# Six plain FFN groups and ten by 7 products, with the attention pairs placed in half steps

## The chip, the cores and the metric

The kernel runs on one core of a Trainium2 chip. Its time is the device time of one execution in microseconds (us); the number of a kernel is the median of several runs. The engines are TensorE (PE, matmuls; PEld is its weight load), VectorE (DVE), ScalarE (ACT), GpSimd (POOL) and SyncE (SP), which here only issues DMA transfers. They run their own instruction lists in order and wait for each other through semaphores. Sixteen DMA engines move data.

## The reference

One layer with gates on x of shape (64, 128, 512), f32, and a context of the same shape:

```python
x = x + tanh(g_xattn) * attention(layernorm(x), ctx, ctx)
x = x + tanh(g_ffn) * ffn(layernorm(x))

# attention: A is a fixed 128x128 matrix of each of 4 heads, summed over all 64 batches, V = ctx @ Wh
O = einsum('hst,bthe->bshe', A, V)
Y = (O - mean) / sqrt(var + 1e-3) * gamma + beta
W = relu(x @ wg_w)
return (W * Y) @ wo_w

# ffn, ternary weights, 512 -> 1408 -> 512
g = (x @ gate_w.T) * gate_s
u = (x @ up_w.T) * up_s
return (silu(g) * u) @ down_w.T * down_s
```

## The kernel before

A tile is one batch of 128 rows by 512, so there are 64 tiles, 32 pairs of tiles (q = 0 to 31) and 16 groups of four tiles. An f32 operand is split into a high and a low f16 part, and a product is made from two or three matmuls.

The first stage (to about 360 us) computes V, the gates W and the sums for A, and stores V and W in scratch memory. A short transition handles the first two pairs of tiles fully. From then on the FFN runs in two stages.

**The plain stage** has NS = 8 groups. Each has 15 steps, n = 15 g + step. Steps 0 to 10 are gate/up steps: `up_mm` issues 8 matmuls for gate and 8 for up of 128 hidden columns (L2067), `silu` on ACT (L907) and `hidden` on DVE (L1436) form the hidden values, `hidden_hi` (ACT, L836) and `hidden_lo` (POOL, L1816) split them. Steps 11 to 14 are down steps: `down_mm` issues 22 matmuls for one tile (L2074) and `finish` on DVE adds the residual. Two PSUM slots alternate between steps: a step on PE waits for `hidden` or `finish` of the step two before.

Beside these steps the rest of the attention is computed, pair by pair, each event of a pair at a fixed step of every engine's list. For pair q: `o` (PE, A times V, L1930), `y_stats` (DVE, L1252) and `y_rstd_pair` (POOL); `y_normal` (ACT); `y_blocks` (DVE, 32x32 transposes), `y_out` (SP, to scratch), `y_in` (SP, back in pieces of 128 bytes, which makes it a whole transpose, L510); `w_load` (SP, L407); `y_pair_affine` (ACT, four instructions, L786); `wy_pair_mul` (DVE, L1284); `wy_pair_hi` (ACT, L825) and `wy_pair_lo` (POOL, L1760), which make the two parts of W * Y; `wo_pair` (PE, 16 matmuls on the high part at L2058, 8 on the low part at L2062); `x1` and `stats2` (DVE, L1295, L1299, L1301); `norm2_pair` (ACT); `x2_blocks` (DVE), `x2_out` and `x1_store` (SP). `v_load`, `v_hi`, `v_lo` bring in V two pairs ahead, `x_again` brings in x. Most of the buffers exist once: `y_in` of a pair waits for the product of the pair before, `w_load` for its `wy_pair_lo`. The FFN groups read x2 back by `x2_in`, again in pieces of 128 bytes.

What sets the places is `pieces(n)`: it lists the pairs and which event (piece 0 to 12) of each is due at step n. Pair q starts at step `first_step(q)`, one every 3.5 steps, rounded down:

```python
def first_step(q):
    return 7 * (q - 3) // 2 + 1 if q > 3 else 2 * q - 6
# piece 0 o, stats, v_hi; 1 normal, v_lo; 2 blocks, v_load; 3 y_out; 4 y_in; 5 w_load; 6 affine
# piece 7 mul, hi, lo, x_again; 9 wo, x1, stats2; 10 norm2; 11 x2_blocks; 12 x2_out, x1_store
```

In the same stage the weights for the second scheme are prepared: eleven times `stage_load`, `stage_residue` (POOL), `stage_store`, one every 8 steps, and six `weights_copy`.

**The stage of 7 products** has NP = 4 pairs of groups. A Strassen-Winograd scheme on 2x2 blocks forms gate and up of two groups by 7 products in place of 8: `seven` issues 28 matmuls for each of the 11 column blocks (loaded as `wbuf`), DVE, ACT and POOL add the products, then 8 tiles of 22 down matmuls follow. `pair_in` loads x2 of a pair of tiles in pieces of 128 bytes, four of them for each pair of groups.

## Time and profile before

| what | value |
|---|---|
| median of the 3 runs | 1440.71 us (1440.6 to 1444.61) |
| span of the profiled execution | 1447.4 us |
| own time of the profiled execution | not given apart from its span |
| PE, DVE, ACT, POOL busy | 98%, 72%, 50%, 51% of the span |
| DMA moved | 324.96 MB, mean 225 GB/s |
| plain stage, from the first gate matmul to the first of the 7 products | about 360 to 1024 us |

The span goes from the first to the last instruction of one execution, and all rows of the trace are from that one. Durations of matmuls in the trace contain the passage through the array (0.38 us for 512 columns), so their pace is read from the starts of rows that follow each other. An "idle before" belongs to the engine and names the work that ended it.

### The profile page before, as it was taken

To read this page: it belongs to the slowest core of one execution; us is meant where nothing else is said; L and a number is where in the kernel's file an instruction comes from. 1 tells how busy PE (TensorE), PEld (TensorE's weight loads), DVE (VectorE), ACT (ScalarE), POOL (GpSimd) and SP (SyncE) were. 2 spreads that over 40 slices of the span, in tenths; PEclk is the share of its full clock that TensorE was granted. 3 is DMA by queue.
4 is the path that set the end of the run, shared out by engine and by line. 5 is a ranking of instruction groups with operands and counts; after the bars stand their busy time and mean duration, and the time that the engine had idled before them with its cause. 6 is when DMAs were issued, how large, how long until landed. Compare 5 with 4: busy or idle time off the path is not lost.

```text
span 1447.4 us, 20320 instructions
## 1 busy us (share of the span) xinstructions
PE 1420.4 (98%) x7097; PEld 728.3 (50%) x7135; DVE 1043.3 (72%) x1562; ACT 726.3 (50%) x1145; POOL 735.3 (51%) x734
## 2 busy tenths in 40 slices
PE   8999999999999999999999999999999999999998
PEld 4666666665445544455444444444444444444443
DVE  7788998878477676766776677564867768768762
ACT  5566565554555635455463545534344444443442
POOL 5656769863564445444553554434137237137235
PEclk9999999999999999999999999999999999999999
DMA  8999898973878796987888897886383473572432
GB/s 275 344 336 306 292 317 318 343 251 130 276 204 263 227 276 206 260 276 210 248 274 237 264 243 222 247 252 164 112 228 115 124 224 122 139 218 98 139 109 89
DMA packets 372920, 324.96 MB, mean 225 GB/s; under 512 B 259280, under 2 KB 285264, under 8 KB 372816
## 3 DMA queue, kind: packets, MB, share of 16 engines
q1 hardware_dynamic: 355248, 291.63, 66.2%
q10 hardware_dynamic: 17568, 31.99, 6.2%
q8 instruction: 59, 0.97, 0.3%
q14 instruction: 45, 0.37, 0.1%
HBM read 209.14 MB, written 114.43 MB: 224 GB/s over the span
## 4 chain that ended last, share of the span: by engine, by line
PE 74%; DVE 10%; DMA 6%; SPq 3%; issue 3%; ACT 2%; POOL 2%; ACTq 0%; DVEq 0%; POOLq 0%
PE ps L2067 24%; PE po L2067 8%; PE pyb L1930 7%; PE ps L2074 7%; PE ptb L2074 5%; PE pyb L2074 5%; PE ps L1988 5%; PE po L1930 3%; PE pyb L2058 3%; PE ptb L2058 3%; DMA wy_scratch<-misc 2%; SPq L510 2%; DVE reg L1129 1%; PE ptb L2062 1%; PE pyb L2062 1%
## 5 line engine op out<-in xcount | busy, mean ns | idle before, releaser
L2067 PE MATMUL ps<-x2t,gate 128*128 128x512 f16 x704 | 166.6, 379 | 1.2 <-DVE tmp L1436 1.1
L1930 PE MATMUL pyb<-xnt,wgs 128*128 128x512 f16 x708 | 166.3, 380 | 1.4 <-DVE wgs L1153 1.3
L2067 PE MATMUL ps<-op,wbuf 128*128 128x512 f16 x704 | 166.3, 379 | 0.5 <-issue 0.5
L2067 PE MATMUL ps<-x2t,up 128*128 128x512 f16 x704 | 166.3, 379 | 0.0
L1800 POOL TENSOR_TENSOR p5b<-p5b,p1b 128x512 f32<-128x512 f32 x44 | 55.7, 1265 | 209.1 <-ACT p5b L860 209.1
L1816 POOL TENSOR_TENSOR hid<-tmp,hid 128x512 f16<-128x512 f32 x88 | 104.6, 1190 | 105.9 <-ACT hid L836 105.9
L2074 PE MATMUL ps<-down_first,hid 128*128 128x512 bf16 x683 | 152.4, 379 | 2.1 <-POOL hid L1816 0.8
L1811 POOL TENSOR_TENSOR hsp<-hall,hsp 128x640 f16<-128x640 f32 (+2 forms) x72 | 123.6, 1731 | 37.1 <-ACT hsp L887 37.1
L2067 PE MATMUL po<-op,wbuf 128*128 128x512 f16 x528 | 129.0, 379 | 0.6 <-DVE u2b L1383 0.6
L1436 DVE SCALAR_TENSOR_TENSOR tmp<-ps,colsb,tmp 128x512 f32<-128x512 f32 x88 | 65.4, 744 | 68.2 <-PE ps L2067 62.3
L1988 PE MATMUL ps<-reg 128*128 128x256 f32 x768 | 109.7, 294 | 4.3 <-DVE reg L1129 3.8
L2067 PEld LDWEIGHTS ps<-op,wbuf 128*128 128x128 bf16 x704 | 68.5, 98 | 84.4 <-issue 2.5
L1760 POOL TENSOR_TENSOR wy_part<-raw,wy_part 128x1024 f16<-128x1024 f32 x30 | 66.0, 2201 | 87.6 <-ACT wy_part L825 87.6
L2067 PEld LDWEIGHTS ps<-x2t,up 128*128 128x128 bf16 x704 | 68.8, 98 | 82.9
L907 ACT ACTIVATE tmp<-ps,colsb 128x512 f32<-128x512 f32 x88 | 60.3, 685 | 99.2 <-PE ps L2067 99.1
L2074 PEld LDWEIGHTS ps<-down_first,hid 128*128 128x128 f16 x704 | 68.1, 98 | 83.4 <-POOL hid L1816 2.0
L2067 PEld LDWEIGHTS ps<-x2t,gate 128*128 128x128 bf16 x704 | 67.0, 98 | 81.0 <-DVE tmp L1436 1.8
L1988 PEld LDWEIGHTS ps<-reg 128*128 128x128 f32 x768 | 98.4, 190 | 13.3 <-DVE reg L1129 5.7
L1930 PEld LDWEIGHTS pyb<-xnt,wgs 128*128 128x128 f16 x708 | 66.4, 98 | 73.7 <-DVE wgs L1153 2.6
L1721 POOL TENSOR_TENSOR reg<-raw,reg 128x512 fp32r<-128x512 f32 x60 | 75.4, 1280 | 39.5 <-ACT reg L706 39.5
L1403 DVE TENSOR_TENSOR nbuf<-po,p1b 128x512 f32<-128x512 f32 x44 | 30.4, 692 | 78.5 <-PE po L2067 78.5
L887 ACT CAST hsp<-hall 128x640 f16<-128x640 f32 (+2 forms) x72 | 48.7, 712 | 71.2 <-PE pyb L2074 36.7
(218 smaller groups left out, 2764.2 us busy)
## 6 DMA issues: line engine op xcount, KB each, us to landing
wbuf<-ws_scratch SPq DMA_DIRECT2D x44, 896.0 KB, 5.0
xr<-in_x SPq DMA_DIRECT2D x62, 512.0 KB, 6.3
raw<-in_ctx_t SPq DMA_DIRECT2D x32, 512.0 KB, 5.6
v_scratch<-tmp ACTq DMA_DIRECT2D x64, 256.0 KB, 6.0
raw<-v_scratch SPq DMA_DIRECT2D x32, 512.0 KB, 6.6
x_scratch<-xr SPq DMA_DIRECT2D x32, 512.0 KB, 4.8
xr<-x_scratch SPq DMA_DIRECT2D x32, 512.0 KB, 5.9
raw<-w_scratch SPq DMA_DIRECT2D x31, 512.0 KB, 6.0
```

Of the source, the lines that this page charges most:

```text
L907: e.activation(tmp[:, m % 3, :], banks[2 * (n % 2)], ACT.Silu, scale=colsb[:, j:j + 1]).then_inc(s["si"])
L1436: e.scalar_tensor_tensor(tmp[:, m % 3, :], banks[2 * (n % 2) + 1], colsb[:, NI + j:NI + j + 1], tmp[:, m % 3, :], ALU.mult, ALU.mult).then ...
L1721: e.tensor_tensor(ct[g % 2][1][:, h, :], raw[:, h, :], f(ct[g % 2][0][:, h, :]), ALU.subtract).then_inc(s["ctlo"])
L1760: e.tensor_tensor(wyt[1][:, :, :], wt_of(q), wyt[0][:, :, :], ALU.subtract).then_inc(s["wylo"])
L1800: e.tensor_tensor(p5b[n % 2][:, :], p5b[n % 2][:, :], p1b[n % 2][:, :], ALU.add).then_inc(s["p15"])
L1811: e.tensor_tensor(hsp[t % 2][1][:, i0:i1, :], hall[:, i0:i1, 128 * i:128 * i + 128], hsp[t % 2][0][:, i0:i1, :], ALU.subtract).then_inc(s[ ...
L1816: e.tensor_tensor(hid[1][m % 11], tmp[:, m % 3, :], hid[0][m % 11], ALU.subtract).then_inc(s["hlo"])
L1930: last = e.matmul(dst, lhs[a], rhs[b], start=(k == 0 and i == 0), stop=(k == n - 1 and i == 2))
L1988: last = e.matmul(ps[t % 2][:, h, :, :], ct[g % 2][i][:, h, 128 * b:128 * b + 128], wh_and_z(q, h, b), start=(n == 0), stop=(n == 2))
L2058: e.matmul(py(t), wyt_of(t)[0][:, k, :], wos[i][k], start=(k == 0 and i == 0), stop=False)
L2067: last = e.matmul(dst, upper(wt), act[i], start=start, stop=stop and exact, skip_group_check=True)
L2074: last = e.matmul(dst, act, packed, start=start, stop=stop and exact)
```

## The change

NS goes from 8 to 6, and with it NP from 4 to 5. Two of the plain groups so move into the scheme of 7 products. The pairs of the attention, as many as before, now start every 2.5 steps. Their events are placed by a table in half steps (`HALVES`, and `SECOND` for pair 2); `pairs_at(event, half)` takes the place of `pieces(n)`. Step n has the halves 2n and 2n + 1. On PE the events of an even half stand in front of the step's matmuls, those of an odd half between gate and up (in a down step, ahead of the second part). On ACT those of an even half now stand ahead of `silu`, those of an odd half behind it. DVE, POOL and SP take both halves of a step together. The staging of weights goes from every 8 to every 6 steps, the copies from every 15 to every 12.

```diff
-NS = 8
+NS = 6
 NP = (NG - NS) // 2
...
-def first_step(q):
-    return 7 * (q - 3) // 2 + 1 if q > 3 else 2 * q - 6
-def pieces(n):
-    return [(q, n - first_step(q)) for q in range(2, B // 2) if 0 <= n - first_step(q) <= 12]
-STAGED = 18
+HALVES = dict(o=0, stats=0, rstd=0, v_hi=1, normal=2, v_lo=2, blocks=3, v_load=3, y_out=4, y_in=6, w_load=7, affine=9, mul=10,
+              x_again=10, hi=11, lo=11, wo=13, x1=13, rstd2=13, norm2=15, blocks2=16, x2_out=17)
+SECOND = dict(blocks=0, y_out=1, y_in=4, w_load=4, affine=9, mul=10, x_again=10, hi=11, lo=11, wo=14, x1=14, rstd2=14, norm2=16,
+              blocks2=17, x2_out=18)
+def half_of(q, event):
+    if q == 2:
+        return SECOND.get(event, -1)
+    if q == 3:
+        return 3 + HALVES[event] + (2 if HALVES[event] >= 6 else 0)
+    return 5 * (q - 4) + 10 + HALVES[event]
+def pairs_at(event, half):
+    return [q for q in range(2, B // 2) if half_of(q, event) == half]
+STAGED = 14
...
             for g in range(NS):
                 for step in range(15):
+                    n = 15 * g + step
...
-                    j, late = divmod(15 * g + step - STAGED, 8)
+                    j, late = divmod(n - STAGED, 6)
                     if 0 <= j < NI and late == 0:
                         stage_load(j)
                     if 0 <= j < NI and late == 3:
                         stage_store(j)
-                    if 1 <= g <= 6 and step == 14:
-                        weights_copy((G1, G2, U2)[(g - 1) // 2], (g - 1) % 2)
-                    for q, piece in pieces(15 * g + step):
-                        if piece == 12:
+                    if n >= 14 and n <= 74 and (n - 14) % 12 == 0:
+                        c = (n - 14) // 12
+                        weights_copy((G1, G2, U2)[c // 2], c % 2)
+                    for half in (2 * n, 2 * n + 1):
+                        for q in pairs_at("x2_out", half):
                             x2_out(q)
                             x1_store(q)
-                        if piece == 3:
+                        for q in pairs_at("y_out", half):
                             y_out(q)
-                        if piece == 2 and 2 < q < B // 2 - 2:
-                            v_load(q + 2)
-                        if piece == 4:
+                        for q in pairs_at("v_load", half):
+                            if 2 < q < B // 2 - 2:
+                                v_load(q + 2)
+                        for q in pairs_at("y_in", half):
                             y_in(q)
-                        if piece == 5:
+                        for q in pairs_at("w_load", half):
                             w_load(q)
-                        if piece == 7:
+                        for q in pairs_at("x_again", half):
                             x_again(q)
...
+            def attention(half):
+                for q in pairs_at("hi", half):
+                    wy_pair_hi(q)
+                for q in pairs_at("v_hi", half):
+                    if q + 1 < B // 2:
+                        v_hi(q + 1)
+                for q in pairs_at("normal", half):
+                    y_normal(2 * q)
+                    y_normal(2 * q + 1)
+                for q in pairs_at("affine", half):
+                    y_pair_affine(q)
+                for q in pairs_at("norm2", half):
+                    norm2_pair(q)
             for g in range(NS):
                 for step in range(15):
+                    n = 15 * g + step
...
+                    attention(2 * n)
                     if step < 11:
                         silu(g, step)
...
-                    for q, piece in pieces(15 * g + step):
-                        if piece == 7:
-                            wy_pair_hi(q)
-                    for q, piece in pieces(15 * g + step):
-                        if piece == 0 and q + 1 < B // 2:
-                            v_hi(q + 1)
-                        if piece == 1:
-                            y_normal(2 * q)
-                            y_normal(2 * q + 1)
-                        if piece == 6:
-                            y_pair_affine(q)
-                    for q, piece in pieces(15 * g + step):
-                        if piece == 10:
-                            norm2_pair(q)
+                    attention(2 * n + 1)
...
-                    for q, piece in pieces(15 * g + step):
...
+                    for half in (30 * g + 2 * step, 30 * g + 2 * step + 1):
+                        for q in pairs_at("blocks2", half):
+                            x2_blocks(2 * q)
+                            x2_blocks(2 * q + 1)
+                        for q in pairs_at("mul", half):
                             wy_pair_mul(q)
+                        for q in pairs_at("v_lo", half):
+                            if q + 1 < B // 2:
+                                v_lo(q + 1)
+                        for q in pairs_at("blocks", half):
+                            y_blocks(2 * q)
+                            y_blocks(2 * q + 1)
+                        for q in pairs_at("stats", half):
+                            y_stats(2 * q)
+                            y_stats(2 * q + 1)
+                        for q in pairs_at("x1", half):
+                            for t in (2 * q, 2 * q + 1):
+                                x1(t)
+                                stats2(t)
...
+            def attention(half):
+                for q in pairs_at("rstd", half):
+                    y_rstd_pair(q)
+                for q in pairs_at("lo", half):
+                    wy_pair_lo(q)
+                for q in pairs_at("rstd2", half):
+                    rstd2_pair(q)
...
+                    n = 15 * g + step
                     if step == 11:
-                        attention(15 * g + 10)
+                        attention(2 * n - 2)
+                        attention(2 * n - 1)
                     if step != 10:
-                        attention(15 * g + step)
+                        attention(2 * n)
+                        attention(2 * n + 1)
...
+            def attention(half):
+                for q in pairs_at("o", half):
+                    o(q)
+                for q in pairs_at("wo", half):
+                    wo_pair(q)
...
                 for which, i in ((0, 0), (0, 1), (1, 0), (1, 1)):
-                    if n == 1 and which and i == 0:
-                        o(3)
+                    if which and i == 0:
+                        attention(2 * n + 1)
...
+                        if part and end == NI:
+                            attention(2 * n + 1)
...
             def first_groups(exact):
                 for g in range(NS):
                     for step in range(15):
-                        for q, piece in pieces(15 * g + step):
-                            if piece == 0 and q > 3:
-                                o(q)
-                            if piece == 9:
-                                wo_pair(q)
+                        attention(30 * g + 2 * step)
                         if step < 11:
                             up_mm(exact, g, step)
                         else:
```

What ACT's list has around a product of a pair of odd number, before (steps 35 to 37; L836 hidden_hi, L907 silu, L786 affine, L815 norm2, L825 hi, L761 v_hi):

```order
L786 ACTIVATE turned<-turned,gb 128x256 [waits s_wyl]
L786 ACTIVATE turned<-turned,gb 128x256 x3
L815 ACTIVATE xn<-xr,nm,rs 128x512 [waits s_x2b,s_nm2]
L815 ACTIVATE xn<-xr,nm,rs 128x512 [waits s_x2b]
L836 CAST hid_65<-tmp 128x512 [waits s_h]
L907 ACTIVATE tmp<-ps,colsb 128x512 [waits s_hlo,s_gm]
L825 CAST wy_part_53<-raw 128x1024 [waits s_wo,s_wm]
L761 CAST reg<-raw 128x1024 [waits s_o,s_vld]
L836 CAST hid_66<-tmp 128x512 [waits s_h]
```

and in the change (steps 37 and 38; L848 hidden_hi, L798 affine, L919 silu, L827 norm2, L837 hi, L773 v_hi; wo of the pair is at the start of step 39 on PE):

```order
L848 CAST hid_66<-tmp 128x512 [waits s_h]
L798 ACTIVATE turned<-turned,gb 128x256 [waits s_wyl]
L798 ACTIVATE turned<-turned,gb 128x256 x3
L919 ACTIVATE tmp<-ps,colsb 128x512 [waits s_hlo,s_gm]
L827 ACTIVATE xn<-xr,nm,rs 128x512 [waits s_x2b,s_nm2]
L827 ACTIVATE xn<-xr,nm,rs 128x512 [waits s_x2b]
L848 CAST hid_67<-tmp 128x512 [waits s_h]
L837 CAST wy_part_53<-raw 128x1024 [waits s_wo,s_wm]
L773 CAST reg<-raw 128x1024 [waits s_o,s_vld]
L919 ACTIVATE tmp<-ps,colsb 128x512 [waits s_hlo,s_gm]
```

Affine stands now directly behind a hidden_hi and in front of silu, and hi stands one step after it directly behind the next hidden_hi; before, a silu and norm2 stood behind affine, and hi came behind the silu of the next step.

What DVE's list has at the same place, before (L1436 hidden, L1284 the product, L1252 y_stats, L1320 x2_blocks, L1234 v_lo):

```order
L1436 SCALAR_TENSOR_TENSOR tmp<-ps,colsb,tmp 128x512 [waits s_um,s_si]
L1284 TENSOR_TENSOR raw<-raw,turned 128x1024 [waits s_wl0,s_aff]
L1252 BN_STATS st<-po 128x6 [waits s_o]
L1254 BN_AGGR mv<-st 128x2 [waits s_st]
L1252 BN_STATS st<-po 128x6
L1254 BN_AGGR mv<-st 128x2 [waits s_st]
L1436 SCALAR_TENSOR_TENSOR tmp<-ps,colsb,tmp 128x512 [waits s_um,s_si]
L1320 STREAM_TRANSPOSE xbuf<-xn 128x512 [waits s_x2s,s_xn2]
L1320 STREAM_TRANSPOSE xbuf<-xn 128x512 [waits s_xn2]
L1234 TENSOR_TENSOR reg<-raw,reg 128x1024 [waits s_vhi]
L1436 SCALAR_TENSOR_TENSOR tmp<-ps,colsb,tmp 128x512 [waits s_um,s_si]
```

and in the change (L1451 hidden, L1299 the product, L1267 y_stats, L1335 x2_blocks, L1249 v_lo, L1288 y_blocks):

```order
L1451 SCALAR_TENSOR_TENSOR tmp<-ps,colsb,tmp 128x512 [waits s_um,s_si]
L1299 TENSOR_TENSOR raw<-raw,turned 128x1024 [waits s_wl1,s_aff]
L1267 BN_STATS st<-po 128x6 [waits s_o]
L1269 BN_AGGR mv<-st 128x2 [waits s_st]
L1267 BN_STATS st<-po 128x6
L1269 BN_AGGR mv<-st 128x2 [waits s_st]
L1451 SCALAR_TENSOR_TENSOR tmp<-ps,colsb,tmp 128x512 [waits s_um,s_si]
L1335 STREAM_TRANSPOSE xbuf<-xn 128x512 [waits s_x2s,s_xn2]
L1335 STREAM_TRANSPOSE xbuf<-xn 128x512 [waits s_xn2]
L1249 TENSOR_TENSOR reg<-raw,reg 128x1024 [waits s_vhi]
L1451 SCALAR_TENSOR_TENSOR tmp<-ps,colsb,tmp 128x512 [waits s_um,s_si]
```

The order of product, y_stats and the next hidden is the same, but the affine that the product waits for (s_aff) is now of the same step; before it was of the step in front. More transposes stand between the hidden instructions.

SP's list between a y_out and the next, in the change (L457 y_out, L486 stage_store, L434 x_again, L519 y_in, L461 x2_out, L438 x1_store, L416 w_load, L402 v_load):

```order
L457 DMA wy_scratch<-misc 128x2x512 [waits s_wyl,s_wyb]
L486 DMA ws_scratch<-stage_83 256x1x512 [waits s_sres]
L434 DMA xr<-in_x 128x1024 [waits s_x1s0]
L519 DMA turned<-wy_scratch 32x32x32 [waits s_wm,s_wys]
L519 DMA turned<-wy_scratch 32x32x32 x3
L461 DMA x_scratch<-xbuf 128x2x512 [waits s_x2b]
L438 DMA x_scratch<-xr 128x1024 [waits s_x1]
L416 DMA raw<-w_scratch 128x4x256 [waits s_wylo]
L402 DMA raw<-v_scratch 128x1024 [waits s_vst1,s_vst0,s_vlo]
L457 DMA wy_scratch<-misc 128x2x512 [waits s_wyl,s_wyb]
```

It is the cycle of before in the same order; one of it now comes every 2.5 steps.

## Rows read from the trace of the kernel before

**Rows 1.** The page: busy time per engine, then busy tenths in 40 slices.
```profile
PE 1420.4 (98%) x7097; PEld 728.3 (50%) x7135; DVE 1043.3 (72%) x1562; ACT 726.3 (50%) x1145; POOL 735.3 (51%) x734
...
DMA  8999898973878796987888897886383473572432
```

**Rows 2.** Windows: busy us of each engine, granted clock, DMA share, GB/s.
```profile
444.90:961.20 516.30, 512.40 (x2480) 252.07 (x2496) 358.98 (x533) 262.87 (x396) 250.72 (x307) 1.00 0.86 248
1236.70:1341.20 104.50, 104.29 (x482) 47.24 (x485) 76.75 (x94) 46.48 (x69) 45.82 (x30) 1.00 0.54 158
1341.20:1445.70 104.50, 101.77 (x469) 46.02 (x472) 56.64 (x84) 39.64 (x61) 40.95 (x29) 1.00 0.34 115
40.00:60.00 20.00, 19.50 (x115) 12.50 (x115) 14.93 (x29) 11.27 (x21) 12.30 (x14) 1.00 1.04 404
580.00:624.00 44.00, 43.88 (x214) 21.66 (x215) 31.63 (x49) 19.66 (x29) 18.80 (x23) 1.00 0.99 279
```

**Rows 3.** Timeline of PE, us 540 to 600: start, us, line, out<-in.
```profile
546.93 1.89 PE L2067 MATMUL ps<-x2t,up 128*128 128x512 f16 x8
548.66 1.89 PE L2058 MATMUL pyb<-wos,wy_part 128*128 128x512 f16 x8
...
552.12 1.03 PE L2062 MATMUL pyb<-wos,wy_part 128*128 128x512 f16 x4
...
560.56 1.78 PE L1930 MATMUL po<-reg,a 128*128 128x256 f32 x12
562.18 1.90 PE L2067 MATMUL ps<-x2t,gate 128*128 128x512 f16 x8
```

**Rows 4.** Timeline, us 615 to 655: PE, then DVE, then ACT.
```profile
616.02 1.03 PE L2062 MATMUL ptb<-wos,wy_part 128*128 128x512 f16 x4
...
616.22 0.75 DVE L1295 SCALAR_TENSOR_TENSOR xr<-pyb,tgx,xr 128x512 f32<-128x512 f32 x1 [1.40 <-PE pyb L2062]
...
619.32 0.18 DVE L1301 BATCH_NORM_AGGREGATE mv<-st 128x2 f32<-128x6 f32 x1
...
621.50 1.23 DVE L1284 TENSOR_TENSOR raw<-raw,turned 128x1024 f32<-128x1024 f32 x1
622.64 0.69 DVE L1252 BATCH_NORM_STATS2 st<-po 128x6 f32<-128x512 f32 x1
...
624.16 0.18 DVE L1254 BATCH_NORM_AGGREGATE mv<-st 128x2 f32<-128x6 f32 x1
625.51 0.75 DVE L1436 SCALAR_TENSOR_TENSOR tmp<-ps,colsb,tmp 128x512 f32<-128x512 f32 x1 [1.16 <-PE ps L2067]
...
619.40 2.07 ACT L786 ACTIVATE turned<-turned,gb 128x256 f32<-128x256 f32 x4
621.39 0.62 ACT L836 CAST hid<-tmp 128x512 f16<-128x512 f32 x1
...
624.30 1.03 ACT L825 CAST wy_part<-raw 128x1024 f16<-128x1024 f32 x1
```

**Rows 5.** Timeline of PE at two waits, and the window after the second.
```profile
408.25 1.04 PE L2062 MATMUL pyb<-wos,wy_part 128*128 128x512 f16 x4 [0.96 <-POOL wy_part L1760]
...
772.14 3.01 PE L2058 MATMUL pyb<-wos,wy_part 128*128 128x512 f16 x8 [2.77 <-ACT wy_part L825]
...
774.00:776.00 2.00, 2.00 (x6) 0.50 0.97 168
```

**Rows 6.** Timeline of SP's DMA issues, us 636 to 790.
```profile
721.56 0.42 SPq L448 DMA_DIRECT2D wy_scratch<-misc  x1
...
728.88 4.65 SPq L510 DMA_DIRECT2D turned<-wy_scratch  x4
...
757.22 6.71 SPq L510 DMA_DIRECT2D turned<-x_scratch  x4
```

**Rows 7.** Groups of instructions, us 367 to 1023.
```profile
L1436 DVE SCALAR_TENSOR_TENSOR tmp<-ps,colsb,tmp 128x512 f32<-128x512 f32 x88 | 65.4, 744 | 68.2 <-PE ps L2067 62.3 <-ACT tmp L907 5.8
...
L1284 DVE TENSOR_TENSOR raw<-raw,turned 128x1024 f32<-128x1024 f32 x30 | 46.4, 1547 | 22.4 <-DMA raw<-w_scratch 21.7
```

30 lines of the change are left out of this document (1 added, 29 removed).

## The prediction

> **What bounds the kernel now.** I read the page first: TensorE is busy for 98% of the span, VectorE for 72%, and the digits of the DMA engines stay between 7 and 9 until late in the program [rows 1]. Then the windows, one for each stage. From 444.9 to 961.2 us (six plain groups with attention between them) PE is busy for 512.4 of 516.3 us, DVE for 359 (70%), and the 16 DMA engines for 0.86 of the time at 248 GB/s. The stage of 7 products takes 104.5 us for a pair of groups, again with a full PE, but its DMA share is only 0.54 and 0.34 [rows 2]. So PE sets the time everywhere, and what differs between the stages is how much cover lies beside it. The timeline of PE gives its pace: 8 matmuls of 512 columns in 1.73 us, 0.2156 us each; o() of a pair in 1.62 us [rows 3]. The waits of PE are short and few: most are like the 0.96 us at 408, and one of 2.77 us at 772 is the long one [rows 5].
>
> **The trade of groups.** Two plain groups go. Each issues 11 x 16 gate and up matmuls and 4 x 22 down matmuls, 264 in all: 264 x 0.2156 = 56.9 us, two are 113.8 us. One pair in the scheme of 7 products comes: 104.5 us by its window [rows 2] (its matmuls alone, 11 x 28 + 8 x 22 = 484, would be 104.3). The difference is **-9.3 us**. The attention of a pair of tiles costs PE 1.62 us for o() and 24 x 0.2156 = 5.17 us for wo_pair(), 6.79 us, and there are as many pairs as before, so nothing is gained or lost there. DVE is busy 76.8 of 104.5 us in a pair [rows 2], so the fifth pair should cost what the third costs. The fewer residuals, stores and x2 loads of the plain stage move to the last stage, where the DMA engines are half idle: nothing.
>
> **The denser attention.** The attention must now fit beside six groups. Fifteen steps carry 6 pairs, not 4.3: 56.9 + 6 x 6.79 = 97.6 us of PE for 15 steps, 16.3 us a pair and not 20. DVE has per pair about 10.9 us of work (v_lo 1.6, the product 1.55, x1 with its statistics 3.3, y_stats 1.7, four transposes 2.8), from the durations in [rows 4, 7]. With 359 us in the six groups for 25.7 pairs, the groups' own part is (359 - 25.7 x 10.9) / 6 = 13 us, and up to 17 us if I add up their rows. That gives 13 to 17 + 65.4 = 78 to 82 us of 97.6, at most 84%. That is no bound by itself. ACT and POOL, at 51% and 49% before, stay below 65%. I cost the loads of these three at nothing on average; what matters is the order within the steps.
>
> **The order within the steps.** Pairs of even number start on a step, odd ones half a step later; the pattern repeats in 5 steps. For a pair of odd number affine (half step 9) now stands on ACT ahead of silu and behind the cast of hidden_hi; its product (10) is in the same step on DVE; hi (11) stands behind the next hidden_hi, and PE wants hi at the very start of the step after that (wo, 13). Before, affine was one step ahead of the product, and wo two whole steps behind hi. I follow the chain from the wo_pair() of the even pair in front. Its first tile is ready 0.2 us before x1 starts; x1 and the statistics take 3.28 us (616.22 to 619.50); then hidden 0.75, the cast 0.53 (it overlaps the next instruction), affine 2.07, the product 1.14 to the next start, y_stats 1.70, hidden 0.75, the cast 0.53, hi 1.03 [rows 4]: 11.98, and some 0.03 at four changes of engine, 12.1 us. PE in that time has 0.86 (second tile) + 1.73 (up) + 5.07 (a step with o) + 3.45 (a plain step) = 11.1 us of work [rows 3]. **PE waits 1.0 us** for tbwh. With the mean of the product, 1.55 us [rows 7], it is 1.4; if DVE has not to wait for the cast in between, it is 0. It happens where all these steps are gate/up steps: the wo at steps 19, 24, 34, 39, 49, 54, 64, 69 and 79, 9 times. In the down steps ACT has no silu or cast and affine runs early. So **+9 us**, between 0 and 13. The pairs of even number have half a step more everywhere: 0, covered by that.
>
> **The start and the staging.** The residues of the seven-product weights now move every 6 steps instead of 8, and the weight copies every 12 instead of 15: the same 22 + 6 transfers, in 410 and not 520 us; they belong to the DMA account below. The first group keeps the places of pairs 2 and 3 nearly as they were. Its PE waits (some 4 us, of which 0.96 at 408) [rows 5] stay. The wait at 772 is a chain through SP's queue; I leave it in, since that chain gets tighter.
>
> **Sum**: span 1447.4 - 9.3 + 9 + 0 = 1447.1. No time of the profiled execution beside its span is shown; the median of the runs, 1440.7, is 6.7 below the span. The same difference on the median gives **1440.4 us**. About 0.3% (4.3 us) is what a measurement of this kernel can tell from no change.
>
> **The DMA account**, the great unknown. The last two windows of pairs differ by three loads of wbuf and four loads of 512 KB in pieces of 128 bytes (pair_in). The last one moves 8 x 0.92 + 8 x 0.52 = 11.5 MB in 0.34 x 104.5 = 35.5 us of all engines, so 1.6 us for 512 KB in large rows; the difference, 20.9 - 8.5 us for wbuf, leaves 3.1 us for one in small pieces [rows 2]. A pair of attention has six of the first and one of the second: 12.7 us. Checked on the six groups: 25.7 x 12.7 + 12 x 3.1 + 24 x 1.6 + 22 x 1.6 + 6 x 2.2 = 449 us, where the window has 0.86 x 516.3 = 444. After the change, in steps 14 to 77 (4.2 groups, 410 us of PE): 25.2 x 12.7 + 8.4 x 3.1 + 16.8 x 1.6 + 35 + 13 = 421, scaled by 444/449 **416 us of DMA in 410 us**, a share of 1.01. Does that fit? A share is a sum of packet times and can pass 1: it was 1.04 for 20 us at 404 GB/s, and 0.99 for 44 us at 279 GB/s in the plain groups while PE missed nothing (43.88 of 44) [rows 2]. So it is at the edge, and I take 0 for it with PE's waits above as slack (each wait gives the queue time too), up to +27 if only 0.95 can be sustained. The Trainium skill, DMA: Bandwidth & Descriptors (Specifications), puts the HBM limit of one core at about 358 GB/s. The account needs some 121 MB in 410 us, 296 GB/s, so by that figure 17% would be free and nothing lost. The trace does not agree in either direction: 404 GB/s were held for 20 us, and in the mixture of small pieces the engines were full at 279. The measurement decides, and the sum keeps its edge.
>
> **The rivals.**
> 1. *The cover holds* (0.34). The 1.0 us of my chain comes from a difference of two sums of 11 and 12 us; if the casts and the product overlap a little more, it is gone. For it: PE lost 4 us in 516 though DVE and ACT were in such chains already. Then only -9.3 is left, and up to 3 us of new small waits: 1431 to 1435, say 1432.
> 2. *The DMA engines and SP's queue become the bound* (0.29): slower. In the plain stage SP issues y_out, waits for it to land (721.56 to 728.88, 7.3 us), then issues y_in (2.8 to 4.65 us), and twice in a group x2_in, up to 6.7 us [rows 6]; with the other issues 13 to 14 us of a period that is now 16.3, and more behind x2_in. From a sustained share of 0.98 down it decides: 416 / 0.98 = 424, 14 us over PE's 410, which cancels 9.3 and passes the 4.3. At 0.96 it is 433, +23 and the waits of my chain lie inside it: 1440.7 - 9.3 + 23 = 1454. For it: the digits of 8 and 9, and the wait of 2.77 us, after which PE ran at the lower of its two clocks, 1.2 GHz (granted 0.50 in 774 to 776; eight matmuls took 3.01 us and not 1.89) [rows 5], so each such wait costs nearly 2 us more. Against it: 0.99 without loss at 580 to 624.
> 3. *The forecast* (0.37): 1436.5 to 1445.
>
> That the change doesn't do what it says is excluded: the counts of matmuls follow from the code.
>
> **Range and chances.** 1431 (rival 1 whole) to 1458 (rival 2 at 0.95); below lies little, above the case of several long waits at the lower clock. The forecast's own range is 1436.5 to 1445. Faster 0.34, same 0.37, slower 0.29.
>
> **What would show it.** The plain stage with attention should hold 543 us of PE work (6 x 56.9 + 30 x 5.17 + 29 x 1.62), in all some 555 to 562; each pair of groups 104.5 us, five times. The chain is right if PE's timeline has waits of about 1 us in front of the first wo matmuls, released by ACT's cast to wy_part, in the steps named and not in between. Rival 1 is right if these are missing and the stage is below 552 us. Rival 2 is right if the DMA share passes 0.95 through the stage, waits of PE lead back to DMA (wy_scratch, w_scratch, v_scratch), and the clock shows stretches at 0.5. I would be wrong in kind if a pair of the last stage takes more than 105 us, or if DVE is busy for over 90% of the stage and PE waits for hidden.

## The result and the profile after

The change takes **1473.7 us** (4 runs, 1471.85 to 1475.48), the kernel before 1442.66 in the same comparison: a ratio of 1.0209, interval 1.0191 to 1.0227. It is 31 us slower. The forecast was 1440.4 with a range to 1458, so both the number and the range missed.

The page of the changed kernel: busy time of the engines, and the DMA engines' share in 40 slices.

```profile
PE 1422.6 (97%) x7091; PEld 724.4 (49%) x7091; DVE 1086.5 (74%) x1613; ACT 741.1 (50%) x1166; POOL 748.9 (51%) x741
...
DMA  7999998973878999998899998275284383483332
```

PE is now busy for 97% of the span, where it was 98% [rows 1]. The windows by stage say where (columns as in [rows 2]: length, busy us of PE, PEld, DVE, ACT and POOL, granted clock, DMA share, GB/s):

```profile
361.00:946.20 585.20, 552.10 (x2653) 268.37 (x2654) 416.12 (x616) 304.87 (x453) 285.62 (x355) 0.98 0.89 260
440.00:890.00 450.00, 422.65 (x2035) 207.07 (x2034) 334.10 (x496) 232.84 (x350) 216.96 (x281) 0.98 0.93 272
...
1050.70:1155.20 104.50, 104.50 (x486) 47.24 (x485) 76.71 (x94) 46.47 (x69) 45.84 (x29) 1.00 0.54 158
...
1364.20:1468.70 104.50, 104.50 (x485) 47.26 (x484) 58.45 (x85) 40.82 (x63) 41.02 (x29) 1.00 0.34 114
```

The plain stage lasts 585 us, where its matmuls are 543.5 us of work at the pace of [rows 3]. The forecast had been 555 to 562. The pairs of groups by 7 products take 104.5 us each, the fifth as the second. So the surprise of this profile is in the plain stage with its dense attention: about 42 us lost there, against some 7 before (664 us for 657 of work). In its middle, DVE is busy for 334 of 450 us, 74%, and the DMA engines have a share of 0.93.

The timeline of PE in that stage (in brackets the idle time before a row and what ended it):

```profile
587.16 1.90 PE L2072 MATMUL pyb<-wos,wy_part 128*128 128x512 f16 x8 [0.83 <-ACT wy_part L837]
...
620.48 3.43 PE L2072 MATMUL pyb<-wos,wy_part 128*128 128x512 f16 x8 [2.63 <-ACT wy_part L837]
...
689.87 1.90 PE L2072 MATMUL pyb<-wos,wy_part 128*128 128x512 f16 x8 [0.88 <-ACT wy_part L837]
...
726.01 3.59 PE L2072 MATMUL pyb<-wos,wy_part 128*128 128x512 f16 x8 [5.45 <-ACT wy_part L837]
...
798.08 3.53 PE L2072 MATMUL pyb<-wos,wy_part 128*128 128x512 f16 x8 [3.31 <-ACT wy_part L837]
```

These are five of 22 waits. They sum to 32 us. Eleven of them, with 22 us, are at the first matmul of a wo_pair, released by ACT's cast wy_pair_hi. Five, at 464, 515, 620, 726 and 798, are 2.6 to 5.5 us long, and behind each PE ran at 1.2 GHz:

```profile
720.50:726.00 5.50, 0.06 (x1) 0.74 0.49 197
726.00:728.00 2.00, 1.99 (x5) 0.50 0.00 0
...
730.00:732.00 2.00, 2.00 (x11) 1.00 1.06 168
```

Behind the wait of 5.45 us the granted clock is 0.50 until about 730. The records of the clock have 20.5 us at this level in the stage, in five stretches. About 4 us of them lie inside the waits themselves (the one around 726 begins at 723); in the rest matmuls of 512 columns take twice 0.2156, which costs another 8 us. Waits of 32 us and 8 us for the clock make 40 of the 42 us.

Behind four of the five long waits (515, 620, 726 and 798) stands a late w_load: the product starts within 0.1 us of its landing. Other products wait for w_load too, without PE waiting behind them. The first line gives the product's waits for w_load in the stage (us in all, times, the longest). Below it stand pieces of the chain that led to the wait at 726 (start, us, what; the last is PE's wo, from the timeline above):

```profile
DVE raw L1299 <- DMA raw<-w_scratch: 27.8, 11, 5.3
...
695.17 1.31 SPq L446
...
697.13 0.40 SPq L402
...
697.62 9.07 DMA wy_scratch<-misc
...
706.72 0.62 SPq L519
...
712.13 0.66 SPq L461
...
712.84 0.47 SPq L438
...
713.35 7.42 DMA raw<-w_scratch
...
720.86 1.22 DVE raw L1299
...
726.01 3.59 PE L2072 MATMUL pyb<-wos,wy_part 128*128 128x512 f16 x8 [5.45 <-ACT wy_part L837]
```

L446 are the two residual loads, L402 is v_load. The y_out behind them took 9.07 us to land. Only then could SP issue y_in (L519), behind it x2_out (L461) and x1_store (L438), and at 713.35 the w_load that the product (L1299) waited for, 7.42 us. So a transfer that does not depend on y_out at all came late because it stands behind y_in in one queue. The wait of 3.10 us at 464 is another matter: its chain runs through an x2_in (landed at 451.7), x1 with its statistics and norm2 on ACT (461.67), with the cast behind it, and e1, e2, e3, e6, e8 and e9 all have it at this place with 3.09 or 3.10 us, the staging or not. SP's own waits in the stage:

```profile
SPq L486 <- POOL stage L1793: 48.9, 7, 9.4
SPq L519 <- DMA wy_scratch<-misc: 47.5, 18, 8.7
```

L486 is the staged block's store, which waits for POOL's residue with y_out or y_in behind it, for up to 9.4 us.

### The profile page after: what moved, and what is told of

The parts are those of the page before. It is cut to its first block, busy times and chain, and to the rows that moved or that the text cites. A ratio compares the mean times of both kernels' runs of the same rounds, so it can differ in the third digit from the quotient of the medians.

```text
span 1473.7 us, 20470 instructions
## 1 busy us (share of the span) xinstructions
PE 1422.6 (97%) x7091; PEld 724.4 (49%) x7091; DVE 1086.5 (74%) x1613; ACT 741.1 (50%) x1166; POOL 748.9 (51%) x741
## 4 chain that ended last, share of the span: by engine, by line
PE 58%; DVE 12%; DMA 12%; SPq 8%; POOL 4%; issue 3%; ACT 3%; ACTq 0%; DVEq 0%
PE ps L2081 15%; PE po L2081 10%; PE pyb L1944 7%; PE ptb L2088 6%; PE pyb L2088 6%; SPq L519 5%; PE ps L2002 5%; DMA wy_scratch<-misc 5%; DMA raw<-w_scratch 2%; PE po L1944 2%; PE ps L2088 2%; PE pyb L2072 1%; DMA xr<-in_x 1%; DVE xr L1140 1%; DVE reg L1144 1%
## 5 line engine op out<-in xcount | busy, mean ns | idle before, releaser
L2081 PE MATMUL ps<-op,wbuf 128*128 128x512 f16 x880 | 207.9, 379 | 0.5 <-issue 0.5
L2081 PE MATMUL ps<-x2t,gate 128*128 128x512 f16 x528 | 124.9, 379 | 2.5 <-DVE tmp L1458 1.3
L2081 PE MATMUL ps<-x2t,up 128*128 128x512 f16 x528 | 124.8, 379 | 0.0
L2088 PE MATMUL ps<-down_first,hid 128*128 128x512 bf16 x528 | 118.0, 379 | 2.0 <-ACT down_first L907 1.0
L2081 PEld LDWEIGHTS po<-op,wbuf 128*128 128x128 bf16 x660 | 64.4, 98 | 78.8 <-DVE u2b L1398 1.1
L2088 PE MATMUL pyb<-down_later,hsp 128*128 128x512 bf16 x440 | 99.0, 379 | 0.0
L2088 PE MATMUL ptb<-down_later,hsp 128*128 128x512 bf16 x440 | 98.2, 379 | 0.0
L848 ACT CAST hid<-tmp 128x512 f16<-128x512 f32 x66 | 40.8, 618 | 109.8 <-DVE tmp L1451 109.7
L1430 DVE SCALAR_TENSOR_TENSOR hall<-nbuf,colsb,tmp 128x512 f32<-128x512 f32 x110 | 84.5, 768 | 8.9 <-ACT tmp L886 2.6
L2072 PE MATMUL pyb<-wos,wy_part 128*128 128x512 f16 x240 | 64.6, 418 | 22.4 <-ACT wy_part L837 22.4
```

The source lines that it names most:

```text
L1430: e.scalar_tensor_tensor(hall[:, j, 512 * half:512 * half + 512], src, colsb[:, NI + j:NI + j + 1], gates, ALU.mult, ALU.mult).then_inc(s[ ...
L2072: e.matmul(py(t), wyt_of(t)[0][:, k, :], wos[i][k], start=(k == 0 and i == 0), stop=False)
L2081: last = e.matmul(dst, upper(wt), act[i], start=start, stop=stop and exact, skip_group_check=True)
L2088: last = e.matmul(dst, act, packed, start=start, stop=stop and exact)
```

## The experiments

The theories. **A**: the order in SP's queue lengthens the chain y_out, y_in, w_load, product. **B**: the DMA engines are full and the bytes are the bound (my second rival). **C**: the chain on ACT and DVE of my forecast. **D** came later: the cycle through the single buffer of w_load. All were run against the kernel before on the same chip; its median was 1442.0 to 1443.3 us in every set, so a difference of 1 or 2 us between two sets tells nothing.

### e1: the residual loads moved

```diff
-                    if step == 4:
+                    if step == 5:
                         residual(2 * g)
+                    if step == 8:
                         residual(2 * g + 1)
```

> The changed kernel with the two residual loads of a group moved from just ahead of a y_out (step 4) to just behind one (steps 5 and 8); nothing else. Theory A (transfer latency on the chain through SP's queue: y_out lands in 9.1 to 9.7 us behind the two residual loads, y_in and w_load stand behind it in the queue, the product comes late and PE waits 2.6 to 5.5 us at wo of pairs 9, 15 and 21, each with a stretch at the low clock): those three waits fall to under 1.2 us and about 15 us are won, 1459 us. Theory B (the 16 DMA engines are full, and the bytes are the bound): the same bytes, so the same time, 1473.7 within 3 us. Theory C (the chain ACT-DVE-ACT of affine, product and hi): the same time.

Measured: 1468.9 us, 5 us won. The waits at pairs 9 and 15 fell from 2.91 and 2.63 to 1.48 and 1.88 us and the clock stayed up; the one at pair 21 fell from 5.45 to 4.10. The y_out of these pairs did land earlier (7.1, 8.1 and 6.4 us for 9.7, 9.2 and 9.1), but at pair 21 issuing y_in then took 7.6 us and not 5.4, and w_load was issued as late as before, 15.5 us behind y_out for 15.7. All waits of PE in the stage still sum to 33 us, since others grew (pair 27 from 1.02 to 1.89); what fell is the time at the lower clock, from 20.5 us to 3.4. Theory A has the direction and a third of the size.

### e2: affine half a step earlier

```diff
-HALVES = dict(..., y_in=6, w_load=7, affine=9,
+HALVES = dict(..., y_in=6, w_load=7, affine=8,
```

> The changed kernel with affine one half step earlier (8, not 9) for every pair from 4 on, so that it no longer stands in the step of its product for pairs of odd number. Theory C (my forecast: PE waits of 0.7 to 1.0 us in front of wo of the odd pairs, from that chain): the five such waits of the profile go, 4 to 5 us are won, up to 9 if the long waits contain it too. Theories A and B: the long waits stay, as y_in or w_load lands too late for the product anyway; at most 1 us, and if y_in is not landed at half 8, ACT is blocked and a few us are lost.

Measured: 1480.3 us, 6.6 slower. The blocked ACT that the last clause spoke of is what happened: affine waits for the late y_in, 69.8 us in all where the change has 16.8, with silu and the casts behind it. PE's timeline has at pair 21, where 5.45 us stood:

```profile
730.64 3.22 PE L2072 MATMUL pyb<-wos,wy_part 128*128 128x512 f16 x8 [7.02 <-ACT wy_part L837]
```

An earlier place does not make an event earlier if its transfer lands late. It only puts more work behind the wait.

### e3: without the staging

The calls of stage_load, stage_store and stage_residue are left out, and weights_in no longer waits for their stores, so the lower halves that the seven-product groups read are not made.

```diff
-                    p.wait_ge("sst", 64 + 16 * NI)
+                    p.wait_ge("sst", 64)
...
-                    if 0 <= j < NI and late == 0:
-                        stage_load(j)
-                    if 0 <= j < NI and late == 3:
-                        stage_store(j)
...
-                    if 0 <= j < NI and late == 2:
-                        stage_residue(j)
```

> The changed kernel without the staging of the seven-product weights: 11 loads and 11 stores of 512 KB and POOL's 11 residues are left out, so the low parts of these weights are not prepared (they are not read when the weights are exact, as here). The DMA account of the stretch falls from 416 to 381 us of 410. Theory B: the bound falls with the bytes, 20 us or more are won and nearly all waits go, 1450 us or less. Theory A: SP is no longer held by the stores that wait for POOL, but the residual loads still stand ahead of y_out, so the three waits at pairs 9, 15, 21 get shorter but stay: 5 to 12 us won.

Measured: 1454.0 us, 19.7 won: more than theory A's 5 to 12, and nearly theory B's 20. Behind the wait of 3.10 us at 461 all waits are regular now, and the product no longer waits for w_load anywhere: it waits for affine, as in my forecast. The middle of the stage, what the product waited for in it, and three waits of PE:

```profile
440.00:890.00 450.00, 432.73 (x2104) 213.72 (x2115) 340.67 (x507) 239.91 (x366) 206.86 (x281) 1.00 0.89 255
...
DVE raw L1295 <- ACT turned L794: 24.0, 9, 2.7
...
578.95 1.90 PE L2066 MATMUL pyb<-wos,wy_part 128*128 128x512 f16 x8 [0.84 <-ACT wy_part L833]
...
610.48 1.90 PE L2066 MATMUL pyb<-wos,wy_part 128*128 128x512 f16 x8 [0.83 <-ACT wy_part L833]
...
633.16 1.04 PE L2070 MATMUL pyb<-wos,wy_part 128*128 128x512 f16 x4 [1.00 <-POOL wy_part L1768]
```

The wait of 0.84 or 0.83 us at 579 and 610 returns (0.83 to 0.85) at wo of eight pairs of odd number, the ninth is 0.67 us: exactly the nine steps of my forecast, 7.4 us in all where I had put 9. Theory C is right and shown cleanly here. A wait of 0.98 to 1.00 us for wy_pair_lo in the down steps, four times, I had not seen. The DMA share is still 0.89, and 21.5 us of waits in all are left.

### e4: dense attention beside eight groups

```diff
-NS = 6
+NS = 8
```

> The changed kernel with eight plain groups and four pairs of groups again (NS = 8) but the dense attention kept, a pair every 2.5 steps. If my trade is right (two plain groups 113.8 us, one pair of groups 104.5), it takes 9.3 us more than the change, 1483 us, and all of the 40 us lost against the first kernel come from the density (all theories). If the trade itself were wrong, it would lie at 1473 or below.

Measured: 1483.2 us, 9.5 more than the change. The trade of groups is worth what its matmuls say, some 9.4 us; the density with its new places costs 40.0 (against 1443.2 in the same set).

### e5 and e13: the even pace, with short gaps and with the old ones

e5 is the new table at a pair every 3.5 steps and eight groups; e13 the same pace and groups with the old gaps, written in half steps (of its edit only the table and the pace are shown; pairs 2 and 3 have places of their own).

```diff
-NS = 6
+NS = 8
-    return 5 * (q - 4) + 10 + HALVES[event]
+    return 7 * (q - 4) + 10 + HALVES[event]
```

```diff
+HALVES = dict(o=0, stats=0, rstd=0, v_hi=0, normal=2, v_lo=2, blocks=4, v_load=4, y_out=6, y_in=8, w_load=10, affine=12, mul=14,
+              x_again=14, hi=14, lo=14, wo=18, x1=18, rstd2=18, norm2=20, blocks2=22, x2_out=24)
...
+    return 7 * (q - 4) + 8 + HALVES[event]
```

> The changed kernel with NS = 8 and the pairs every 3.5 steps as in the first kernel, but placed by the new table of half steps: the placement alone. If the loss is from the density (theories A and B), this is the first kernel's time within 4 us, 1439 to 1447 us. If the new places (affine beside the product, events in front of silu) cost by themselves (theory C at any pace), it is over 1447.

> Eight groups and a pair every 3.5 steps, as in the run at the even pace (1523 us), but with the gaps between the events of a pair as in the first kernel, written in half steps: y_out to affine 3 steps and not 2.5, w_load to product 2 and not 1.5, y_out to wo 6 and not 4.5. If the short gaps are what cost at the even pace, 1440 to 1450 us. If the half steps themselves cost (events in front of silu, wo between gate and up), it stays over 1460.

Measured: e5 **1523.1 us**, 80 us slower than the kernel before, and e13 **1451.9 us**, 9 slower. Both do the work of the kernel before, at its pace and with its bytes; between them the gaps, and with them the order of the events in every list, differ. e5 has the lowest DMA share of all. SP's waits, then the window in its middle:

```profile
SPq L461 <- DVE xbuf L1335: 97.6, 18, 12.9
SPq L519 <- DMA wy_scratch<-misc: 65.5, 20, 9.0
...
440.00:890.00 450.00, 406.62 (x1882) 193.93 (x1894) 271.45 (x404) 199.04 (x303) 181.44 (x233) 0.95 0.78 231
```

And its engines' waits:

```profile
DVE xr L1310 <- PE pyb L2076: 83.5, 21, 6.1
...
PE pyb L2072 <- ACT wy_part L837: 50.3, 21, 6.1
...
DVE raw L1299 <- ACT turned L798: 29.7, 22, 4.6
```

SP stands 98 us in front of x2_out, since at this pace it comes ahead of y_out and its transposes (half step 16) just before it. PE waits 50 us for the operand of wo, 21 times, most often 1.51 or 3.0 us. But no transfer is late here: neither affine nor the product has a wait for y_in or w_load, w_load landed 0.2 to 12.5 us before each product, and the median y_out took 4.1 us to land, where the kernel before has 6.9. Two waits of x1 for x, 10.8 us, are the only ones of these events on a transfer. What PE waits for is a chain of the engines. Pieces of the one that ends in the wait of 3.02 us at 996.20:

```profile
984.58 0.02 ACT tmp L919
...
985.17 1.04 ACT reg L773
986.20 1.00 ACT xn L827 x2
...
987.52 0.60 ACT hid L848
988.13 1.34 ACT nbuf L792 x2
989.47 1.97 ACT turned L798 x4
...
992.61 1.30 DVE misc L1288 x2
993.91 0.64 DVE tmp L1451
...
995.10 1.05 ACT wy_part L837
```

The table of half steps gives the reason, as far as a trace can tell; no run moves these events apart and keeps the gaps. Seven half steps on, normal (2) of the next pair falls on affine (9) and its blocks (3) on mul (10), and norm2 (15) and v_hi (1) fall just ahead of affine (8). So behind one silu ACT has v_hi, norm2, hidden_hi, y_normal and affine in a row, then DVE the product, y_blocks and hidden, and only then comes the cast for wo: 11.6 us from 984.58 to 996.15, in which PE has 8.6 us of work. With the period of 5 of the change, and in e13's table, normal and blocks of the neighbour don't fall on affine and mul. This is theory C's mechanism, and the second clause of what I expected of e5 (over 1447 if the new places cost by themselves) is the one that came true. The same stretch of e13:

```profile
440.00:890.00 450.00, 446.00 (x2175) 219.78 (x2174) 326.62 (x468) 226.79 (x342) 216.84 (x268) 1.00 0.88 256
```

PE is busy for 446 of 450 us at a share of 0.88, where e5 has 407 at 0.78. The slower run has the emptier DMA engines. But since e5 is slow for a reason of its own, neither it nor its distance from e13 tells what transfers cost in the change. Of the 9 us between e13 and the kernel before, its profile shows three longer waits of PE (2.29, 3.19 and 2.58 us at 372, 423 and 853), each with 3.4 us at the lower clock; the first two lie in the first group, with its new start. It was not taken apart further.

### e6, e11 and e7: what of the staging costs

e6 keeps loads and stores but leaves out POOL's residues; a store waits for its load. e11 leaves out the transfers, with e3's cuts in SP's list, and keeps 11 POOL instructions of the same size on another buffer. e7 does all the work, with the store later. In this order:

```diff
-                p.wait_ge("sres", residues("stage", j))
+                p.wait_ge("sld", 16 * (j + 1))
...
-                    if 0 <= j < NI and late == 2:
-                        stage_residue(j)
```

```diff
-                p.wait_ge("sld", 16 * (j + 1))
-                residue(stage[j % 2][:, :, :, :].rearrange("p k o n -> p (k o n)"))
+                residue(down[:, 0:2, :].rearrange("p i n -> p (i n)"))
```

```diff
-                    if 0 <= j < NI and late == 3:
+                    if 0 <= j < NI and late == 5:
                         stage_store(j)
```

> The changed kernel with the staging's loads and stores kept but POOL's 11 residues left out, and each store waits only for its own load (the low parts of these weights are not prepared; they are not read here). All bytes stay, SP is no longer held by POOL. Leaving the whole staging out gave 20 us. Theory A (the order in SP's queue: y_out and y_in stand behind a store that waits for POOL for up to 9.4 us): most of the 20 us come here, 1456 to 1460 us. Theory B (bytes): nothing or the little that POOL's 22 us give, 1470 us or more.

> The changed kernel without the staging's loads and stores but with 11 POOL instructions of the same size at the same places of its list (on another tile; the low parts of the seven-product weights are not prepared, they are not read here). Beside the run without staging (1454.0) and the one with the bytes alone (1459.5). If the staging costs through its bytes, this is 1454 to 1457; if POOL's 22 us cost (lo and rstd come later, and w_load waits for lo), 1462 to 1468 us.

> The changed kernel with the store of a staged block two steps later (5 steps behind its load, not 3); the same work in full. POOL does the residue at step 2, so the store should find it done. Theory A: SP's waits on POOL's residue (48.9 us) go, 10 us or more are won, 1455 to 1464 us. Theory B: no change, 1473 within 3 us.

Measured: 1459.5 (e6, as theory A had said), 1459.3 (e11), 1470.6 (e7, 3 us won, close to theory B's case). Against 1454.0 without any of it, the bytes alone cost 5.6 us and POOL's 22 us alone 5.3, yet both together and the store's wait 19.7. The window of e6:

```profile
440.00:890.00 450.00, 429.00 (x2075) 211.42 (x2086) 337.87 (x502) 237.09 (x360) 200.78 (x275) 0.99 0.95 279
```

This is the highest share, 0.95 at 279 GB/s, in a run 14 us faster than the change. Theory B as a bound falls with it: with all bytes moved the stage can be 14 us shorter. Some 6 us of the loss do come with these transfers. Theory A falls short too: in e7 SP no longer waits for POOL's residue, and the wait only moves on:

```profile
SPq L519 <- DMA wy_scratch<-misc: 55.4, 19, 9.3
...
SPq L416 <- POOL wy_part L1772: 21.4, 9, 4.1
```

L416 is w_load, which waits for wy_pair_lo, and L519 y_in, which waits for y_out to land. Taking one wait out of this chain uncovers the next; that this is why the parts of the staging cost more together than one by one is my reading, no run shows it alone.

### e9: w_load from ACT's queue

The function is the same, called in ACT's list at half step 7; the call in SP's list is left out.

```diff
+            def w_load(q):
+                p.wait_ge(*(("tbwe", 2) if q == 2 else ("wylo", q - 2)))
...
+                e.dma_start(wt_of(q), w_s[q // 2, :, :, 256 * (q % 2):256 * (q % 2) + 256]).then_inc(s[f"wl{q % 2}"], 16)
...
+                for q in pairs_at("w_load", half):
+                    w_load(q)
```

> The changed kernel with w_load issued from ACT's own queue (half step 7, behind the wait for the wy_pair_lo of the pair before), so that it no longer stands behind y_in, x2_out and x1_store in SP's queue. Theory A (order in SP's queue; in the long waits the product starts as soon as w_load lands): the five long waits and their stretches at the low clock go, 1450 to 1458 us. Theory D (the cycle w_load, product, hi, lo, next w_load through the one buffer is the limit): w_load waits for lo on ACT instead, ACT is held, at most 5 us won. Theory B (bytes): no change.

Measured: 1469.4 us, 4 won, as theory D said. The longest waits are gone (one of 3.09 us, the others 2.8 at most), with more of 0.8 to 2.5 in their place: all waits of PE in the stage sum to 37 us, 4 more than in the change. What was won is the clock, which stayed up through the whole stage, behind the 3.09 us too.

### e12: wo and what follows half a step later

```diff
-..., lo=11, wo=13, x1=13, rstd2=13, norm2=15, blocks2=16, x2_out=17)
+..., lo=11, wo=14, x1=14, rstd2=14, norm2=16, blocks2=17, x2_out=18)
```

A second line, not shown, keeps pair 3 where it was; e14 to e19 have it too.

> The changed kernel with wo, x1, rstd2, norm2, x2_blocks and x2_out one half step later for every pair, all before wo left where it is: 3.3 us more between the product and wo. Theories A and D with DVE as the sufferer (its list stands behind the product that waits for w_load): the waits move to the gate matmuls and the down matmuls (released by hidden), and little is won, 1465 to 1473 us. If PE alone waited for the late operand, all waits under 3.3 us go and the low clock with them: 1448 to 1455 us.

Measured: 1456.7 us (1451.6 to 1461.8), 17 won, close to the second case. Here nothing was left out, only the place of six events changed, and the loss against the kernel before fell from 31 to 13.4 us. All bytes are moved, at a share of 0.94 in the same 450 us and so again higher than the change's 0.93, which speaks against theory B more directly than e6 does, where POOL's work is gone too. What is left has moved to the matmuls of gate and down, which wait for hidden (L1451) behind a late product on DVE. One such wait of PE (2.05 us, and the lower clock behind it), and SP's wait of x_again for x1_store, which now stands two half steps ahead of it:

```profile
713.43 3.38 PE L2081 MATMUL ps<-x2t,gate 128*128 128x512 f16 x8 [2.05 <-DVE tmp L1451]
...
SPq L434 <- DMA x_scratch<-xr: 66.2, 22, 4.9
```

### e8, e14 to e19: the parts together

e8 has the moves of e1 and e7, and wo, x1 and rstd2 half a step later for the pairs of odd number:

```diff
-    return 5 * (q - 4) + 10 + HALVES[event]
+    return 5 * (q - 4) + 10 + HALVES[event] + (q % 2 if event in ("wo", "x1", "rstd2") else 0)
```

> The changed kernel with the later store of the staged block, the residual loads behind y_out as in the first experiment, and wo, x1 and rstd2 of the pairs of odd number half a step later, between gate and up. Theory A for the first two: the sum of both, about 1456 us. Theory C for the third: the 0.83 us in front of wo of 9 odd pairs, seen clean in the run without staging, go as well, another 7 us: 1446 to 1450 us. If theory C is wrong, the 9 waits stay, now in front of the wo half a step later.

e8 took 1465.3 us. Of the waits of 0.83 us in front of wo few are left (0.93, 1.16 and 0.60 us, beside the 3.09 of the start), as theory C said, but 3.56, 3.39 and 2.77 us stand in front of the down and gate matmuls, which wait for hidden: the sum does not come.

The next four have the table of e12 (in e16 with wo and what follows another half step later) but x_again at 11, behind y_in. e14 and e16 add the moves of e1 and e7, e15 also that of e9; e17 only leaves out the staging. The table of e14:

```diff
-..., x_again=10, hi=11, lo=11, wo=14, ...
+..., x_again=11, hi=11, lo=11, wo=14, ...
```

> The run with wo half a step later, with three transfers moved: x_again half a step later (11, behind y_in), the staged block's store two steps later, the residual loads behind y_out (steps 5 and 8). Same bytes, same arithmetic. Order theory: SP's waits on x1_store (66 us) and on POOL's residue go, 5 to 12 us more are won, 1445 to 1452 us. Byte theory: 1456.7 within 3 us.

> The run above with w_load from ACT's queue. In the run with the later wo, the product still came late at the odd pairs (PE waits of 1.4 to 2.1 us for hidden, which stands behind it on DVE). If w_load's place behind y_in in SP's queue does that, these go and 3 to 6 us more are won, 1440 to 1448; if it is the cycle through the one buffer, no more than 2 us.

> As e14, with wo and all behind it one more half step later (15, a full step behind the change). If PE still waits for the operand of wo, this takes the rest away: 3 us or more below e14. If the waits are at hidden by then (DVE behind the late product), it is equal to e14 within 2 us, or slower, as hi of the next pair has to wait for wo on ACT.

> The run with the later wo (and x_again behind y_in), without the staging (the low parts of the seven-product weights are not prepared; they are not read here). Order theory: little is left to win once e14 is ordered, so this is within 4 us of e14. Byte theory: it is well below e14, at the time of full PE, 1436 to 1442 us, that is below the kernel before.

Measured: 1475.6 (e14), 1475.6 (e15), 1500.3 (e16), 1462.3 (e17): all slower than e12, even e17, without the 11.5 MB of the staging. That e14 would be slower was not expected; e15 equals it, as was expected if the cycle through the one buffer is the limit; and e16 is slower still, as its last clause said: hi waits 26.9 us for wo in four waits, and the product 71.9 us for w_load. The engines' waits of e14 have a new one, x1 for x:

```profile
DVE xr L1311 <- DMA xr<-in_x: 46.2, 15, 7.1
```

x_again stood behind y_in, which waits some 9 us for y_out, and then had three half steps to land. The last two put it back to 10, and e19 against e14 shows what that half step costs: nothing else differs between them, and it is 21.6 us. e19 is e12 with the moves of e1 and e7; e18 also has x1_store at a place of its own (half step 16, behind y_in).

```diff
-              x_again=11, hi=11, lo=11, wo=14, x1=14, rstd2=14, norm2=16, blocks2=17, x2_out=18)
+              x_again=10, hi=11, lo=11, wo=14, x1=14, rstd2=14, norm2=16, blocks2=17, x2_out=18, x1_store=16)
...
-                            x1_store(q)
...
+                        for q in pairs_at("x1_store", half):
+                            x1_store(q)
```

> The run with wo half a step later (1456.7), x_again left at 10, with x1_store at a place of its own (half step 16, behind the next y_in, ahead of x2_out at 18), the staged block's store two steps later and the residual loads behind y_out. SP's 66 us of waits on x1_store in front of x_again and y_in go. If the queue's order is what is left: 1445 to 1452 us. If it is the bytes or the cycle through the single buffers: 1454 us or more.

> The same without the new place of x1_store: the run with the later wo, the staged block's store two steps later and the residual loads behind y_out. Alone on the change these gave 3 and 5 us. If they add: 1449 to 1453 us; the slow runs e14 and e17 are then due to x_again alone.

Measured: 1458.8 (e18, 1452.6 to 1459.2) and 1454.0 us (e19; ratio to the kernel before 1.0076, interval 1.0059 to 1.0093). x1_store at its own place wins nothing. e19 is the best version in full found, 20 us below the change and 12 above the kernel before; the moves add 3 us at most to e12, whose own runs lie between 1451.6 and 1461.8. No run here beats the kernel before.

## Why the prediction was wrong

- **The trade of groups, -9.3 us**: right. e4 and the change differ by 9.5 us, and the pairs of groups take 104.5 us, five times.
- **The order within the steps, +9 us**: right as a mechanism, with the nine steps, and 7.4 us in size, read from e3. In the change itself it is hidden in part under longer waits.
- **The DMA account**: its number was right, 416 us of DMA; the middle of the stage has 0.93 x 450 = 418. The step that failed is the next sentence of it, "I take 0 for it with PE's waits above as slack, up to +27 if only 0.95 can be sustained". It priced the transfers by the share of the engines. What they cost is a matter of when one lands: the product waited 27.8 us for w_load, 11 times, four of the long waits of PE stand behind it, and e3, with the staging's transfers and POOL's residues gone, has no such wait and wins 19.7 us.
- **The rest of the 33 us.** On the spans 26.6 us were missing, 1473.7 against 1447.1: the stage lost 42 us, and the forecast had in it 9 and the 7 of the profile before. The other 6.7 are what I took off between the span of that profile and the median; the changed kernel's span is equal to its median. And with the late w_load gone, e3 still has 21.5 us of waits where I had counted some 13: the 3.1 us at 461 and the four of 1 us for wy_pair_lo were not in the sum.
- **The second rival** had the sign and the waits' addresses (SP's queue, y_out, w_load), and the low clock behind the long waits. Its deciding point, a sustained share under 0.98, was the wrong quantity: e6 and e12 are faster at 0.95 and 0.94 than the change at 0.93. I had read the two numbers that matter, y_out to y_in 7.3 us and a cycle of 13 to 14 us [rows 6], but compared them with the period of 16.3 us, a matter of rate, and not with the gap that is left between a transfer and its use.
- The gaps in us are what I should have worked out. From y_out to wo the kernel before had 6 steps of 20/3.5 = 5.7 us, 34 us; the new table has 4.5 steps of 6.5, 29 us. Even that is too much, since y_out is issued late within its step: at pair 21 from 697.62 to 720.56, when PE was free for wo, 22.9 us. In it had to fit, by the chain shown above, 9.1 us for y_out, 6.6 until w_load was issued, 7.5 until it landed, and the product, hidden_hi and the cast behind them, 28.4 us in all. The difference is the wait of 5.45. That a longer gap helps in the change is shown by e12 (17 us). e5, with the same table and 4.5 x 5.7 = 26 us, can't be counted for it: its transfers were in time.
- **Rival 1** (the cover holds) is excluded by the 32 us of waits. Its plus, that chains had held before, did not carry over to the new places: at the old pace the new table loses 80 us (e5), and one with the old gaps 9 (e13).
- **Range**: the upper end took the share of 0.95 as the worst. It lacked that long waits would also cost clock, 8 us in all here; I had said so of one wait in rival 2 but not multiplied it.

What stays open: why the late transfers cost as much as they do once several meet (5.6 and 5.3 us alone, 19.7 together), and how much of the loss left in e12 and e19 is the new places themselves and how much the cycle w_load, product, hi, lo, next w_load. A second buffer for it would tell; it wasn't tried, so this is left open.

## What to carry to other kernels

When a schedule of fixed places is compressed, work out for each transfer the time in us between its issue and its use and compare it with its landing time under load, with all that stands ahead of it in its queue; a sum of loads per engine, even a right one, does not see it. Then, for the new period, write down which events of neighbouring pairs fall on the same step of one engine: in e5, with y_in and w_load in time for every pair, PE still waited 50 us for wo's operand behind such a chain. A transfer that waits in an in-order queue behind an unrelated one has that one's latency too. If PE waits, first try the consumer later (six entries of a table won 17 us here) before taking work away, and expect that an event placed earlier than its data only blocks its engine (e2). Moving a load has the same risk: x_again half a step later, behind a y_in that waits, cost 21.6 us.

## What the runs showed of the hardware

- y_out of 512 KB took 9.07 us to land behind two residual loads and a v_load, and 6.4 us at the same pair without the two ahead of it (e1); its median rose from 6.9 us before (445 to 961) to 7.6 (367 to 946), and that of a stage_load from 6.6 to 7.7. In e5, at a DMA share of 0.78, it was 4.1.
- In the change, waits of PE of 2.6 to 5.5 us were each followed by a stretch at 1.2 GHz, and those of up to 1.3 us were not. The length of a wait doesn't settle it: 3.09 us (e1 and e9) and 2.79 us (e9) were not, 2.05 us (e12) and 2.29 us (e13) were. The change has 20.5 us of it in the stage, e5 some 55 us in all.
- Costs of parts did not add: 5.6 and 5.3 us alone, 19.7 us together with the wait between them.
- The windows of this kernel sustained a DMA share of 0.95 at 279 GB/s over 450 us (e6), in a mixture where three of four packets are under 512 bytes (186832 of 249143 in the plain stage of the change).
